# Routed LoRA and expert kernel on Trainium2: the last slot's code in a branch of its own with f32 mixing, W's tile first, and the slots' low parts on VectorE

## The chip, the cores and the metric

The kernel runs on one core of one Trainium2 chip. The metric is the time of one execution on the device in microseconds (us), the median of several runs. Five engines work side by side, each with an instruction queue of its own, and meet by semaphores only: TensorE (PE; PEld is its weight load), VectorE (DVE), ScalarE (ACT), GpSimd (POOL) and the sync engine (SP), which issues most transfers. PEq, DVEq, ACTq, POOLq and SPq stand for the queues themselves, where registers are computed, semaphores waited for and branches taken.

## The reference

The input x holds 32 batches of 64 tokens of 1024 features, f32. Four layers add to it in turn:

```python
x = x + einsum('bct,bcd->bdt', x, W0[cond])           # 16 tables of 64x64, over the 64 tokens
x = x + einsum('bct,bcd->bdt', x, W1[cond])           # the same kind of table
x = x + x @ W.T + (x @ A[labeler]) @ Bw.T * 0.5       # a 1024x1024 base and a low-rank part
x = x + einsum('bsi,boi->bso', x, weight[adapter])    # one of 8 matrices of 1024x1024 for each batch
```

The tables mix tokens and the matrices mix features, so both mixings commute with the feature layers: the kernel computes layers 3 and 4 on the raw x and mixes the 64 tokens of each batch last, with one 64x64 table per condition, (I+W0)(I+W1). Every f32 operand is cut in a high and a low part of reduced precision (`F32R`, fast on TensorE), and a product is three matmuls: high by high, high by low, low by high.

## The kernel before

**Start and base layer.** Transfers bring x and W in tiles of 128 rows. ScalarE writes the high part of each (`x_hi`, `w_hi`), VectorE the low part (`x_lo`, `w_lo`: tile minus high part, L831 and L838). For the first block this goes tile by tile: in the SP block the tile of x is issued before that of W (L281, L282), ScalarE makes `x_hi` then `w_hi` (L595, L597), VectorE adds the unit matrix to a block of W (L1086), then `x_lo`, then `w_lo`. TensorE warms up with `WARM` = 20 matmuls (L1257), computes the table of mixings from f32 operands of 64 rows (L1265), then layer 3 (`main`, L1286 to L1288, one line for each of the three products).

**A plan made on the chip.** VectorE sorts the batches by adapter and packs two batches of the same adapter in a slot. A word per slot in `plan` holds its batches, whether it has a single one (`SINGLE`), whether adapter tiles are to be loaded in it and where. There are between `SURE` = 16 and `SLOTS` = 20 slots; the number is read at run time as `n_slots`. For these inputs it is 17, and slots 4 and 16 hold a single batch.

**Slots.** For slot i the engines do, in `step(i)`:
- ScalarE: `rows_hi(i-1)` (high part of the last slot's result, L694), `slot_hi(i+1)` (high part of the next slot's x, L685), `adapter_part` (high parts of up to 8 adapter tiles, L671), `mixed_cols(i-1)` (L706).
- VectorE: `rows_lo(i-1)` (L1166), `adapter_part` (low parts, L1149), `mixed_sum(i-1)` (L1177).
- GpSimd: `slot_lo(i+1)`, the low part of the next slot's x (L429, two of 128x512), then `mixers(i)` (L443, L445), then the unit matrix on adapter tiles that have landed (L421).
- TensorE: eight tiles of 128 rows, each three products (two for a single slot) for each of two halves of 512 columns (L1400). Between the halves of the tiles comes `mix(i-1)` (L1427), the token mixing of the slot before: four matmuls, for two tables and two halves. Each part stands in `pe.If(single < 1)` / `pe.Else()` (L1411, L1431), so the code of both kinds of slot lies in the queue, one behind the other.
- SP: the transfers of adapter tiles (L332), then `store(i-1)` (L351).

**Slots from `ENDS` = 15 on** can be the last one. TensorE then goes half by half of the columns: all tiles of the first half, `mix(i-1)`, seven tiles of the second (`MIX_AT`), `mix_last(i, 0)` if this is the last slot, the eighth tile, and after the last slot `mix_last(i, 1)` (L1446). `mix_last` needs high and low parts of the slot's result: `last_hi` (L769) on ScalarE and `last_lo` (L1214) on VectorE, two each for a half. Its products are gathered by `last_cols` (L798) and `last_sum` (L1236), and stored in halves of columns and of rows from SP (L368) and ScalarE (L785). Work for slots that may not exist stands in nested branches:

```python
for i in range(SURE, SLOTS):
    with pe.If(n_slots == i):
        mix_last(i - 1, earlier[2], 1)
    nested.enter_context(pe.If(n_slots > i))     # L1489; DVE L1245, ACT L808, SP L394, POOL L496
    earlier, mine = slot(i, earlier, mine)
```

With 17 slots the first of these conditions holds and the second does not: the queue jumps over the code of slots 17, 18 and 19 to the end. Behind its own jump SP waits for every store, L401 and L403. What lies at L248 is the end of a queue's program, with a drain.

## Time and profile before

| | |
|---|---|
| time, median of 3 runs | 394.82 us (394.56 to 395.0) |
| profiled execution | 394.66 us, span of its instructions 392.9 us |
| TensorE, VectorE, ScalarE, GpSimd busy | 380.2, 268.3, 231.2, 123.3 us |
| start to first product; slots; after the last slot's products | 0 to 9.5; 186.9 to 382.5; 382.5 to 392.9 us |
| granted TensorE clock, mean | 0.992 |

The span runs from the first to the last instruction of the traced program. All times of rows are in us from its start, durations marked as such in ns. In a timeline or chain row the first number is the start, the second the time until the last instruction of the group ends; `x4` is the number of instructions. Matmuls overlap each other in such rows: a row's length is more than their number times the step from one to the next. `[3.30 <-DVE aT L1214]` says that the engine was idle for 3.30 us before the row and which instruction ended that. A row of a source line lists durations as min/median/max in ns.

### The profile page before, as it was taken

To read this page: it belongs to the slowest core of one execution; us is meant where nothing else is said; L and a number is where in the kernel's file an instruction comes from. 1 tells how busy PE (TensorE), PEld (TensorE's weight loads), DVE (VectorE), ACT (ScalarE), POOL (GpSimd) and SP (SyncE) were. 2 spreads that over 40 slices of the span, in tenths; PEclk is the share of its full clock that TensorE was granted. 3 is DMA by queue.
4 is the path that set the end of the run, shared out by engine and by line. 5 is a ranking of instruction groups with operands and counts; after the bars stand their busy time and mean duration, and the time that the engine had idled before them with its cause. 6 is when DMAs were issued, how large, how long until landed. Compare 5 with 4: busy or idle time off the path is not lost.

```text
span 392.9 us, 7604 instructions
## 1 busy us (share of the span) xinstructions
PE 380.2 (97%) x1736; PEld 316.4 (81%) x1736; DVE 268.3 (68%) x285; ACT 231.2 (59%) x307; POOL 123.3 (31%) x163
## 2 busy tenths in 40 slices
PE   8999999999999999999999999899999999999990
PEld 8888888888888888888888887688888888888860
DVE  4746967865855958547967439953699546899563
ACT  3798859387232775244483549554677357777361
POOL 0000340100003000024865427763258434576400
PEclk9999999999999999999999999999999999999996
DMA  7984902740348475406526224742276322762223
GB/s 225 396 313 158 375 3 79 261 180 19 107 173 288 182 277 166 180 21 214 175 93 221 58 55 123 260 133 55 56 235 211 97 57 56 270 219 54 56 58 88
DMA packets 24219, 61.37 MB, mean 156 GB/s; under 512 B 1938, under 2 KB 2066, under 8 KB 24146
## 3 DMA queue, kind: packets, MB, share of 16 engines
q1 hardware_dynamic: 23808, 60.30, 46.1%
q8 instruction: 28, 0.46, 0.5%
q14 instruction: 45, 0.37, 0.3%
q10 hardware_dynamic: 338, 0.24, 0.2%
HBM read 52.15 MB, written 8.39 MB: 154 GB/s over the span
## 4 chain that ended last, share of the span: by engine, by line
PE 96%; issue 1%; DVE 1%; ACT 0%; POOL 0%; ACTq 0%; DVEq 0%; POOLq 0%
PE ps L1400 44%; PE ps L1286 13%; PE ps L1287 13%; PE ps L1288 13%; PE ps L1427 4%; PE ps L1313 4%; PE ps L1325 2%; PE ps L1257 1%; PE ps L1265 1%; DVE stage L1236 0%; DVE stage L1177 0%; ACT stage L706 0%; DVE aT L1214 0%; PE ps L1446 0%; ACT stage L798 0%
## 5 line engine op out<-in xcount | busy, mean ns | idle before, releaser
L1400 PE MATMUL ps<-ring,aT 128*128 x784 | 180.8, 389 | 0.0
L1400 PEld LDWEIGHTS ps<-ring,aT 128*128 128x128 f32 x784 | 147.1, 188 | 30.8 <-issue 0.4
L1286 PE MATMUL ps<-ring 128*128 128x512 f32 x224 | 88.3, 394 | 0.0
L1287 PE MATMUL ps<-ring 128*128 128x512 f32 x224 | 88.0, 393 | 0.0
L1288 PE MATMUL ps<-ring 128*128 128x512 f32 x224 | 87.9, 392 | 0.0
L429 POOL TENSOR_TENSOR aT<-xT,aT 128x512 fp32r<-128x512 f32 (+1 forms) x36 | 56.3, 1585 | 51.3 <-ACT aT L685 45.2
L1149 DVE TENSOR_TENSOR ring<-raw,ring 128x1024 f32 (+1 forms) x40 | 63.8, 1655 | 5.1 <-ACT ring L671 5.0
L694 ACT ACTIVATE aT<-ps 64x1024 fp32r<-64x1024 f32 x32 | 32.7, 1021 | 48.1 <-PE ps L1400 47.6
L1177 DVE TENSOR_TENSOR stage<-ps,stage 64x1024 f32<-64x1024 f32 x30 | 36.7, 1222 | 26.3 <-ACT stage L706 25.7
L1166 DVE TENSOR_TENSOR aT<-ps,aT 64x1024 fp32r<-64x1024 f32 x32 | 39.1, 1222 | 22.6 <-ACT aT L694 21.9
L1288 PEld LDWEIGHTS ps<-ring 128*128 128x128 f32 x224 | 42.6, 190 | 9.0
L1286 PEld LDWEIGHTS ps<-ring 128*128 128x128 f32 x224 | 42.6, 190 | 8.9
L1287 PEld LDWEIGHTS ps<-ring 128*128 128x128 f32 x224 | 42.6, 190 | 8.7
L706 ACT ACTIVATE stage<-ps 64x1024 f32<-64x1024 f32 x30 | 30.5, 1017 | 23.7 <-PE ps L1427 23.3
L671 ACT ACTIVATE ring<-raw 128x1024 f32 (+1 forms) x40 | 39.4, 1046 | 8.3 <-POOL raw L421 6.0
L562 ACT ACTIVATE xT<-ps 128x512 f32<-128x512 f32 x40 | 22.6, 592 | 23.0 <-PE ps L1288 22.0
L421 POOL TENSOR_TENSOR raw<-raw,eye 128x128 f32<-128x128 f32 x40 | 19.5, 497 | 24.9 <-DMA raw<-w3t 20.1
L451 POOL TENSOR_TENSOR ring_f<-ring_f,eye 128x128 f32<-128x128 f32 x8 | 5.5, 724 | 66.7 <-DVE ring_f L900 49.6
L838 DVE TENSOR_TENSOR ring<-ring_f,ring 128x1024 fp32r<-128x1024 f32 (+1 forms) x20 | 21.9, 1127 | 5.2 <-ACT ring L513 5.1
L513 ACT ACTIVATE ring<-ring_f 128x1024 fp32r<-128x1024 f32 (+1 forms) x20 | 18.5, 965 | 6.8 <-DMA ring_f<-xt 5.1
L451 POOL TENSOR_TENSOR xT<-xT,eye 128x128 f32<-128x128 f32 x4 | 7.6, 1932 | 44.6 <-DVE xT L894 44.6
L685 ACT ACTIVATE aT<-xT 128x512 fp32r (+1 forms) x36 | 19.9, 599 | 2.4 <-DVE xT L911 2.1
(82 smaller groups left out, 314.5 us busy)
## 6 DMA issues: line engine op xcount, KB each, us to landing
raw<-w3t SPq DMA_DIRECT2D x40, 512.0 KB, 4.4
ring_f<-xt SPq DMA_DIRECT2D x8, 1024.0 KB, 7.7
raw<-xt SPq DMA_DIRECT2D x8, 1024.0 KB, 5.1
out<-stage SPq DMA_DIRECT2D x30, 256.0 KB, 3.0
ring_f<-wt SPq DMA_DIRECT2D x4, 1024.0 KB, 7.4
xT<-xt SPq DMA_DIRECT2D x3, 1024.0 KB, 9.5
xT<-wt SPq DMA_DIRECT2D x2, 1024.0 KB, 15.2
ring_f<-xt SPq DMA_DIRECT2D x4, 256.0 KB, 6.4
```

Source lines behind the costliest of these rows:

```text
L429: pool.tensor_tensor(x3_split(i, ks, P + h * T, T), xT[:, ks, bass.ds(which[h] * T, T)], as_f32(x3_split(i, ks, h * T, T)), ALU.subtract). ...
L562: act.activation(dst[:, o, :], ps_l2(phase, j, o), ACT.Copy).then_inc(s(name), 1)
L671: act.activation(dst, adapter_raw(t), ACT.Copy).then_inc(s("w_hi"), 1)
L694: act.activation(r_tile(h)[own, :], acc(i)[own, :, :].rearrange("p a n -> p (a n)"), ACT.Copy)\
L706: act.activation(stage[own, i % 2, :], mixed_ps[h][other, :, :].rearrange("p a n -> p (a n)"), ACT.Copy)\
L1149: dve.tensor_tensor(in_two(unit_of(t, 1)), adapter_raw(t), as_f32(in_two(unit_of(t, 0))), ALU.subtract)\
L1166: dve.tensor_tensor(r_tile(h)[other, :], acc(i)[own, :, :].rearrange("p a n -> p (a n)"), as_f32(r_tile(h)[own, :]), ALU.subtract).then_in ...
L1177: dve.tensor_tensor(dst, mixed_ps[h][own, :, :].rearrange("p a n -> p (a n)"), dst, ALU.add)\
L1286: pe.matmul(dst, hi_of(qw)[:, k, cs], hi_of(qx)[:, k, :], start=start and k == 0, stop=False, skip_group_check=True)
L1287: pe.matmul(dst, hi_of(qw)[:, k, cs], lo_of(qx)[:, k, :], start=False, stop=False, skip_group_check=True)
L1288: last = pe.matmul(dst, lo_of(qw)[:, k, cs], hi_of(qx)[:, k, :], start=False, stop=stop and k == HALF - 1, skip_group_check=True)
L1400: last = pe.matmul(acc(i)[:, n, :], x3_split(i, k, start, P), ring[:, bass.ds(off + (part * D + n * 512), 512)], start=(k == 0 and j == 0) ...
```

## The change

1. **W's tile first.** SP issues the tile of W before that of x, ScalarE makes `w_hi` before `x_hi`, and VectorE `w_lo` before `x_lo`, for the four tiles of the first block.
2. **Low parts of x on VectorE.** `slot_lo` leaves GpSimd. VectorE makes slot 0's in two parts around `c12(1)`, slot 1's behind the first adapter's tiles, and slot i+1's in `step(i)` directly behind `rows_lo(i-1)`.
3. **The last slot in a branch of its own.** On each engine a recursive `rest` replaces the nested branches: `If(n_slots > i+1)` holds the step and all that is deeper, its `Else` the last slot's code. Slot 15 is an ordinary slot when it isn't the last. In the last slot TensorE goes by three parts of the columns (512, 256, 256), once for pairs (`columns(PAIR)`) and once for single slots (`columns(ALONE)`).
4. **f32 mixing of the last slot.** GpSimd puts the tables together in one f32 matrix, ScalarE copies the result in f32 (`last_row`), and one f32 matmul for each part mixes it, with no low parts, column copies or sums behind it. `last_row` lies where the rows of slot i-1 are, so the first copy waits for their mixing. Six matmuls (`BRIDGE`) stand before the last one.
5. **Stores and waits.** In a single last slot there are three stores, of one part each and all rows, the last one from ScalarE. Each `store(i)` waits for `store(i-2)`, and the row of waits at the end goes.

The core of the diff (the same pattern of `rest` on ScalarE and VectorE is left out, and what is only taken away):

```diff
             for k in range(HALF):
                 one = slice(k, k + 1)
+                sp.dma_start(raw_of(w_slot(0))[:, one, :], w_block(1, 1)[:, one, :]).then_inc(s(f"w_in0_{k}"), 16)
                 sp.dma_start(raw_of(x_slot(0))[:, one, :], x_block(1, 0)[:, one, :]).then_inc(s(f"x_in0_{k}"), 16)
-                sp.dma_start(raw_of(w_slot(0))[:, one, :], w_block(1, 1)[:, one, :]).then_inc(s(f"w_in0_{k}"), 16)
...
+    END_COLS = (slice(0, 512), slice(512, 768), slice(768, D))
...
             def store(i, word):
                 rows, single = batches(word), get(word, SINGLE)
+                if i >= 2:
+                    sp.wait_ge(s(f"stored{i - 2}"), 32)
                 sp.wait_ge(s("staged"), 2 * (i + 1))
...
+                sp.wait_ge(s(f"stored{i - 2}"), 32)
                 with sp.If(single < 1):
...
                 with sp.Else():
-                    first = slice(0, T // 2)
-                    for n in range(2):
-                        sp.wait_ge(s("end_staged"), n + 1)
-                        sp.dma_start(out_half(rows[0], n, first), stage[first, i % 2, 512 * n:512 * (n + 1)]).then_inc(s("end"), 16)
+                    for part in range(2):
+                        sp.wait_ge(s("end_out"), part + 1)
+                        store_part(0, part, "end")
+                sp.wait_ge(s(f"stored{i - 1}"), 32)
...
-            for i in range(SLOTS - 1):
-                if i < SURE - 1:
-                    sp.wait_ge(s(f"stored{i}"), 32)
-                else:
-                    with sp.If(n_slots > i + 1):
-                        sp.wait_ge(s(f"stored{i}"), 32)
-            sp.wait_ge(s("end"), 64)
+            def rest(i, word):
+                if i == SLOTS:
+                    store_last(i - 1, word)
+                    return
+                with sp.If(n_slots > i):
+                    rest(i + 1, step(i, word))
+                with sp.Else():
+                    store_last(i - 1, word)
+            rest(SURE, word)
+            sp.wait_ge(s("end"), 48)
...
         def _(pool):
+            def mixers_last(word):
...
+                with pool.Else():
+                    whole(slice(0, P), cs[0], slice(0, T)).then_inc(s("end_st"), 3)
...
         def _(act):
+            def last_rows(i, part):
+                act.wait_ge(s("end_left"), part + 1)
+                act.activation(last_row[:, END_COLS[part]], end_acc(i, part), ACT.Copy).then_inc(s("end_rows"), 1)
+            def last(i, earlier, word):
+                rows_hi(i - 1)
+                act.wait_ge(s("mixed"), i)
+                last_rows(i, 0)
+                mixed_cols(i - 1, earlier)
+                last_rows(i, 1)
+                last_rows(i, 2)
+                act.wait_ge(s(f"stored{i - 2}"), 32)
+                act.wait_ge(s("end_mixed"), 3)
+                act.activation(stage[:, i % 2, END_COLS[2]], end_ps(i, 2), ACT.Copy).then_inc(s("end_out2"), 1)
+                act.wait_ge(s("end_out2"), 1)
+                act.dma_start(out_part(batches(word)[0], 2), stage[0:T, i % 2, END_COLS[2]]).then_inc(s("end"), 16)
...
         def _(dve):
             adapter_lo((0, HALF), 0, lambda t, part: unit(KT + t, part))
-
+            word = slot_word(dve, 0)
+            slot_lo(0, word, (0, HALF))
             c12(1)
+            slot_lo(0, word, (HALF, KT))
             adapter_lo((HALF, KT), 0, lambda t, part: unit(t - HALF, part))
+            slot_lo(1, slot_word(dve, 1))
...
             def step(i, earlier, word):
-                following = slot_word(dve, i + 1) if i + 1 < SLOTS else None
+                following = slot_word(dve, i + 1)
                 if i:
                     rows_lo(i - 1)
+                    slot_lo(i + 1, following)
...
+            def last(i, earlier):
+                rows_lo(i - 1)
+                mixed_sum(i - 1, earlier)
+                dve.wait_ge(s(f"stored{i - 2}"), 32)
+                for part in range(2):
+                    dve.wait_ge(s("end_mixed"), part + 1)
+                    dve.tensor_copy(stage[:, i % 2, END_COLS[part]], end_ps(i, part)).then_inc(s("end_out"), 1)
...
         def _(pe):
+            def mix_last(i, part):
+                pe.wait_ge(s("end_st"), 3)
+                pe.wait_ge(s("end_rows"), part + 1)
+                pe.matmul(end_ps(i, part), last_mix[:, :], last_row[:, END_COLS[part]], start=True, stop=True)\
+                  .then_inc(s("end_mixed"), 1)
...
+                def columns(passes):
+                    end_products(i, mine, passes, 0)
+                    mix(i - 1, earlier[2])
+                    end_products(i, mine, passes, 1)
+                    mix_last(i, 0)
+                    end_products(i, mine, passes, 2, (0, END_AT))
+                    mix_last(i, 1)
+                    end_products(i, mine, passes, 2, (END_AT, KT))
+                slot_ready(i)
+                with pe.If(mine[2] < 1):
+                    columns(PAIR)
+                with pe.Else():
+                    columns(ALONE)
+                warm(BRIDGE, acc(i - 1)[:, 1, 256:512])
+                mix_last(i, 2)
+            def rest(i, earlier, mine):
+                if i == SLOTS - 1:
+                    last_slot(i, earlier, mine)
+                    return
+                with pe.If(n_slots > i + 1):
+                    rest(i + 1, *slot(i, earlier, mine))
+                with pe.Else():
+                    last_slot(i, earlier, mine)
...
-            for i in range(SURE):
+            for i in range(ENDS):
                 earlier, mine = slot(i, earlier, mine)
...
+            rest(ENDS, earlier, mine)
```

`PAIR` is ((0, 0), (0, 1), (P, 0)), `ALONE` ((T, 0), (T, 1)), `END_AT` 6.

## Rows read from the trace of the kernel before

**Rows 1.** The page, part 1: busy time, share of span and number of instructions.

```profile
PE 380.2 (97%) x1736; PEld 316.4 (81%) x1736; DVE 268.3 (68%) x285; ACT 231.2 (59%) x307; POOL 123.3 (31%) x163
```

**Rows 2.** Waits of PE: in total, times, longest, us.

```profile
PE ps L1427 <- issue: 1.8, 3, 1.5
```

**Rows 3.** Timeline of PE from 370 us on: start, length, instructions, idle time before.

```profile
377.24 1.18 PE L1427 MATMUL ps<-aT,st 128*128 128x512 f32 x4 [0.17 <-issue]
378.26 3.35 PE L1400 MATMUL ps<-ring,aT 128*128 x14
...
385.81 0.85 PE L1446 MATMUL ps<-aT,st 128*128 128x512 f32 x2 [3.30 <-DVE aT L1214]
```

**Rows 4.** The same view for all engines, 364 to 393 us: ScalarE and VectorE.

```profile
378.51 1.21 ACT L769 ACTIVATE aT<-ps 64x512 fp32r<-64x512 f32 x2 [2.97 <-PE ps L1427]
...
379.75 2.07 ACT L706 ACTIVATE stage<-ps 64x1024 f32<-64x1024 f32 x2
380.81 2.48 DVE L1177 TENSOR_TENSOR stage<-ps,stage 64x1024 f32<-64x1024 f32 x2 [0.26 <-ACT stage L706]
```

**Rows 5.** SP's last stores by source line: durations, first and last start; time to landing.

```profile
L368 SPq DMA_DIRECT2D out<-stage x2: 342/362/381, 385.9 to 388.4; - x2
...
DMA to landing us min/median/max: 2.5/2.7/2.8
```

**Rows 6.** Branches, SP's waits and its drain, by source line.

```profile
L1489 PEldq COMPARE_BRANCH  x2: 68/2034/3999, 370.3 to 385.8; - x2
...
L394 SPq COMPARE_BRANCH  x2: 40/45/50, 374.3 to 388.8; - x2
...
L401 SPq EVENT_SEMAPHORE  x7: 28/28/28, 391.3 to 391.7; - x7
...
L248 SPq DRAIN  x1: 13/13/13, 392.7 to 392.7; - x1
```

**Rows 7.** Timeline of the start, VectorE and PE.

```profile
5.92 3.68 PE L1265 MATMUL ps<-stage 64*128 64x64 f32 x32
...
8.37 0.69 DVE L831 TENSOR_TENSOR ring<-ring_f,ring 128x512 fp32r<-128x512 f32 x1
...
9.53 0.79 PE L1286 MATMUL ps<-ring 128*128 128x512 f32 x1
```

**Rows 8.** Timeline of VectorE, low parts of adapter tiles in slots 4 and 14.

```profile
237.67 5.75 DVE L1149 TENSOR_TENSOR ring<-raw,ring 128x1024 f32 x4 [0.83 <-ACT ring L671]
...
354.41 6.88 DVE L1149 TENSOR_TENSOR ring<-raw,ring 128x1024 f32 x4
```

**Rows 9.** Timeline of PE: matmuls of 256 columns at the full clock.

```profile
137.45 4.00 PE L1313 MATMUL ps<-ring,a_sel 128*128 128x256 f32 x32
```

**Rows 10.** The tensor queue in 366 to 371, 354.9 to 357.9, 371 to 374 us.

```profile
L1411 PEldq COMPARE_BRANCH  x5: 65/179/292, 366.8 to 370.7; - x5
...
L1400 PEldq FUSED_REGOPS  x16: 46/46/51, 355.3 to 357.5; - x16
...
L1400 PEldq FUSED_REGOPS  x16: 42/46/51, 371.3 to 373.9; - x16
```

**Rows 11.** The chain that ended last: start and length of slot 14's and 15's products.

```profile
356.22 10.88 PE ps L1400 x48
```

**Rows 12.** Transfers of PE's instructions (q8), 255 to 360, 387 to 388, 390 to 391 us.

```profile
q8 instruction: 10, 0.16, 0.6%
...
q8 instruction: 1, 0.02, 5.8%
...
q8 instruction: 1, 0.02, 7.5%
```

**Rows 13.** Timeline of VectorE before slot 15's rows.

```profile
374.53 2.48 DVE L1166 TENSOR_TENSOR aT<-ps,aT 64x1024 fp32r<-64x1024 f32 x2 [2.74 <-ACT aT L694]
```

**Rows 14.** PE at 14.3 us; one microsecond by engine, clock after POOL, DMA share, GB/s.

```profile
14.32 0.40 PE L1288 MATMUL ps<-ring 128*128 128x512 f32 x1
...
386.00:387.00 1.00, 0.66 (x2) 0.10 (x1) 0.00 (x0) 0.13 (x1) 0.00 (x0) 0.64 0.89 275
```

More of the change, by code:

```diff
@@ L242, in build, with out_part @@
     BEFORE3, WBASE = HALF, HALF * OPERANDS
-    def out_half(row, n, rows=slice(0, T)):
-        return out[bass.ds(row, 1), rows, 512 * n:512 * (n + 1)].rearrange("a t d -> (a t) d")
+    def out_part(row, part, rows=slice(0, T)):
+        return out[bass.ds(row, 1), rows, END_COLS[part]].rearrange("a t d -> (a t) d")
     with nc.Block() as block:
@@ L489, in step, with rest @@
                 return word, following
+            def rest(i, earlier, word):
+                if i == SLOTS - 1:
+                    mixers_last(word)
+                    return
+                with pool.If(n_slots > i + 1):
+                    rest(i + 1, *step(i, earlier, word))
+                with pool.Else():
+                    mixers_last(word)
             earlier = None
-            for i in range(SURE):
+            for i in range(ENDS):
                 earlier, word = step(i, earlier, word)
-            with contextlib.ExitStack() as nested:
-                for i in range(SURE, SLOTS):
-                    nested.enter_context(pool.If(n_slots > i))
-                    earlier, word = step(i, earlier, word)
+            rest(ENDS, earlier, word)
         @block.scalar
@@ L771, in last @@
-            def last(i, word):
-                rows, single = batches(word), get(word, SINGLE)
-                last_cols(i, single, 0)
-                last_hi(i, 1)
-                last_cols(i, single, 1)
-                with act.If(single < 1):
-                    for n in range(2):
-                        act.wait_ge(s("end_staged"), 2 * n + 2)
-                        act.dma_start(out_half(rows[1], n), stage[T:P, i % 2, 512 * n:512 * (n + 1)]).then_inc(s("end"), 16)
-                with act.Else():
-                    second = slice(T // 2, T)
-                    for n in range(2):
-                        act.wait_ge(s("end_staged"), n + 1)
-                        act.dma_start(out_half(rows[0], n, second), stage[second, i % 2, 512 * n:512 * (n + 1)]).then_inc(s("end"), 16)
@@ L1250, in _, with rest @@
+            def rest(i, earlier, word):
+                if i == SLOTS - 1:
+                    last(i, earlier)
+                    return
+                with dve.If(n_slots > i + 1):
+                    rest(i + 1, *step(i, earlier, word))
+                with dve.Else():
+                    last(i, earlier)
+            earlier = None
+            for i in range(ENDS):
+                earlier, word = step(i, earlier, word)
+            rest(ENDS, earlier, word)
         @block.tensor
@@ L1387, in slot_record, with products @@
                         get(word, SINGLE))
-            def products(i, mine, passes, tiles, ns, first):
+            def products(i, mine, passes, tiles):
                 count8, offs, _ = mine
@@ L1473, in slot, with end_products @@
                     mix(i - 1, earlier[2])
-                    slot_part(i, mine, (0, MIX_AT), (1,), False)
-                    with pe.If(n_slots == i + 1):
-                        mix_last(i, mine[2], 0)
-                    slot_part(i, mine, (MIX_AT, KT), (1,), False)
+                slot_part(i, mine, (HALF, KT))
                 return mine, following
+            def end_products(i, mine, passes, part, tiles=(0, KT)):
+                count8, offs, _ = mine
+                cols = END_COLS[part]
+                for k in range(*tiles):
+                    if part == 0:
+                        pe.wait_ge(s("w_lo"), count8 + (k + 1 + WBASE - KT))
+                    off = offs[k // HALF] + (k % HALF) * UNIT
+                    for j, (start, split) in enumerate(passes):
+                        last = pe.matmul(end_acc(i, part), x3_split(i, k, start, P),
+                                         ring[:, bass.ds(off + (split * D + cols.start), cols.stop - cols.start)],
+                                         start=(k == 0 and j == 0), stop=(k == KT - 1 and j == len(passes) - 1))
+                if tiles[1] == KT:
+                    last.then_inc(s("end_left"), 1)
```

223 lines of the change are left out of this document (72 added, 151 removed).

## The prediction

> **What bounds the kernel now.** I read the page first: the matmul engine is busy for 380.2 of 392.9 us [rows 1], so only its idle stretches and what lies after its last instruction can be won. The waits name 1.8 us ahead of the slots' mixing, 1.5 of them in one piece [rows 2]. The timeline of the end has the rest: products and mixing run nearly without a gap up to 382.5 (after the row at 378.26 come two mixing matmuls and the last two products), then TensorE idles 3.3 us until two matmuls at 385.81 [rows 3]. In that pause ScalarE and VectorE make high and low parts of the last 512 columns, in turns, as the pair at 378.51 shows for the first 512 [rows 4]. Last, the sync queue: its last store is issued at 388.4 and lands some 2.7 us later, at about 391.1 [rows 5]. The span goes on to 392.9, and the branch records tell why: after the branch over the unused slots (L394, 388.8) the next instruction starts at 391.3. This 2.5 us is no wait for data; the seven waits there take 28 ns each. The tensor queue has such a branch too, L1489: 68 ns when it falls through, 3999 ns when it jumps over the three unused slots [rows 6]. A far jump costs 2.5 us on SP and 4.0 us on PE. Today all of them are taken after the last work.
>
> The profiled execution took 394.66 us, span 392.9 and 1.8 around it, 0.16 under the median of 394.82. I sum changes of the span and add them to the median.
>
> **The start.** W's tile first swaps two pairs of equal steps: the second low part still ends at about 9.06 (8.37 and 0.69). The first product starts at 9.53, when the mixing table's f32 matmuls are through (5.92 and 3.68), and not for it [rows 7]: cover 0.5 us, cost 0.0.
>
> **The slots.** A low part of 128x512 costs VectorE 0.69 us [rows 7], so a slot adds 1.38 us there, behind `rows_lo`, ahead of adapter tiles and of `mixed_sum`. Most slots have that room. The tight ones are those with four adapter tiles. In slot 4 these ran from 237.67 for 5.75 us (1.24 each where nothing disturbs, as the sums of [rows 4], 5.0 in all), and the chain behind them gave the 1.5 us stall. There VectorE had idled 0.83 us, so the cost is 0.55 us less contention that leaves with GpSimd's work, at most 0.8. In slot 14 no idle time precedes the group and it takes 6.88 us [rows 8]; 1.38 come in, up to 1.9 go out, but GpSimd's casts move forward into it. I take 0 for both; ends -0.3 and +1.3.
>
> **The tail, code at hand.** The last slot is a single one: 16 products of one half (14 and 2 around the mixing in [rows 3]). Part 0 and the mixing of slot 15 stay as they are, ending at 378.26. Part 1 is 16 matmuls of 256 columns, 0.125 each (4.00/32) [rows 9]: 380.3. The f32 mixing matmul is not in the trace at this size. Nearest is L1265: 32 of 64 rows and 64 columns in 3.68 us at the half clock [rows 7]. If two half-height ones run side by side, 512 columns of full height cost 0.92 us at the full clock; the other end is 0.23, as the reduced-precision ones. I take 0.92, and 0.46 for 256: 381.2. Twelve products, the second mixing and four products: 383.6. ScalarE copies 256 columns in 0.38 (0.60 for 512, 1.03 for 1024, [rows 4]): 384.2 with 0.2 to start. Last mixing with 0.35 ahead: 385.0; copy 385.6; issued 385.8, landed 388.5, end 388.9. This replaces 385.81 to 388.2 and removes two low parts, two sums and 1.2 us of waits on SP. The six bridging matmuls (0.75) lie in ScalarE's copy.
>
> SP has a longer chain. Slot 15's sums ended at 383.29; ScalarE now has one copy of 0.59 ahead of them, not 1.21: 382.67. From there to SP's first last store were 2.6 us (two stores of slot 15) [rows 4, 5]. **But the branch over unused slots now stands before `store_last`, since that is in its `Else`, behind all deeper slots' code.** With 2.55 us for it the first store goes at 387.8, the second at 388.3, lands at 391.0, end 391.4: 1.5 us better than 392.9.
>
> **The same branch on PE.** In slot 15, after the mixing, the tensor queue begins the second half at 366.8 [rows 10]. A half of 24 products passes the queue in 3.1 us (355.3 to 357.5 for its address steps, and the branches around them), so it reaches the branch at 370.0, 3.4 us ahead of the engine: 24 x 0.227 (10.88/48, [rows 11]), from 368.0 behind the four mixing matmuls at 367.1, ends at 373.4. The branch takes 4.0 us [rows 6]: 374.0. From a branch to the first product's address step were 1.0 us (370.3 to 371.3) [rows 6, 10], and 0.2 to the matmul: 375.2, 1.8 us late.
>
> Then, 0.4 us behind, comes a second jump: over `columns(PAIR)` to `columns(ALONE)`. In the slots blocks of 16 KB of instructions came once in 10.5 us (10 in 105 us) [rows 12], and a slot of 11.8 us (10.88 and the mixing's 0.91) holds both branches, 80 products and 8 mixing matmuls. `PAIR` has 72 products and 6 others: some nine tenths of a block. So the target lies nearly always in the next block. After the jump at 385.8 the next block began to come only between 390 and 391 [rows 12], 4.8 us after the branch, 0.8 after PE went on. The first block's transfer began between 387 and 388 [rows 12], and PE went on at 389.8, so a block is ready some 2.3 us after its transfer begins. That makes about 7.3 us after the first branch: 377.3; with 0.7 for the address steps and the load, first product 378.0, 4.6 us late. The ends: the block is there (1.8 late), or a full load of 4.0 from 374.4 (5.7 late). I take 4.6, which follows the only far jump in the trace.
>
> On this the Trainium skill speaks against the change: "Runtime: NRT & Kernel Launch", section "Instruction fetch mechanics", says that a taken branch to outside the two loaded pages stalls until its page has come. By that both of PE's jumps are charged. The trace agrees for the first, with 3999 ns. The same section gives PE 128 KiB; if that much were kept ahead, the second would be free, which is the first rival.
>
> The other engines take the jump in idle time: VectorE idles 2.74 us before slot 15's rows at 374.53 [rows 13], ScalarE waits for the same products before them, and what GpSimd has to make is due at 380.
>
> **The clock.** TensorE stood 3.3 us before 385.81, and within the next microsecond the granted clock fell from 2.4 GHz to 1.2 GHz, 0.64 on the mean [rows 14]. A pause of 4.6 us is longer. At the start the first product took 0.79 at 9.53 and one took 0.40 at 14.3 [rows 7, 14]: half rate for 4.8 us, 2.4 us lost. So the last slot loses between 0 and 2.4 us; I take 1.0, as it may not fall, and what it costs behind slot 15's mixing is hidden by SP's chain, 2.5 us longer than PE's.
>
> **The sum.** Mixing of slot 15 starts at 381.6 (378.0 + 16 x 0.227), not 377.24: 4.4 late. SP's chain 391.4 + 4.4 + 1.0 = 396.8, against 392.9: +3.9, **398.7 us**.
>
> **The rivals.** (a) One load: PE's second jump finds its block. 1.8 late at the first product, 1.6 at the mixing: 391.4 + 1.6 = 393.0, time 394.9. For it: jumps over half a slot cost 0.07 to 0.3 us throughout. Against: these blocks had long been loaded.
> (b) The other side: no load delays PE, because the queue runs far enough ahead. SP's alone remains: 391.4, time 393.3. It decides at 2.2 us: a branch that costs less than that leaves the engine fed. Against it: 4.0 in the only row; for it: at 370 no transfers stand before the block, at 386 stores did.
> (c) The change does as it says, no load in any path: 388.9, time 390.8. It needs SP's 2.5 us gone too.
> (d) Two full loads and a clock that falls: +1.1 and +1.4 on the forecast, 401.2. For it: the jump may start its own load.
> (e) VectorE as the bound in slots: +1.3 at most, on top of any.
> The point between slower and faster is a mixing of slot 15 that starts 1.5 us late (392.9 - 391.4).
>
> **How the numbers follow.** Two loads 0.60 (with (d)), one load 0.14, (b) 0.17, (c) 0.06, the rest something else. A measurement tells 0.2%, 0.8 us, from no change. (a) lies within it with its spread of 0.8 to each side: half of its chance same, the rest to both sides. Faster 0.27, same 0.10, slower 0.63. The range leaves out (c) and the top of (d): 392.8 to 400.6. The likeliest case alone: 396.8 to 401.2.
>
> **What would show it.** Right: a branch in the tensor queue of some 4 us at about 370, the matmul engine idle from 373.4, a second long one at the branch between `PAIR` and `ALONE`; SP's 2.5 us now between slot 15's stores and the last ones; the granted clock below 1 in the last slot. The 1.5 us stall in slot 5 about as long as now. Wrong: no idle time at 373, both branches below 0.4 us; then (b) or (c). Wrong in size: f32 mixing matmuls of 0.25 us, or a stall ahead of the mixing of slots 4, 9 or 14 that grew.

## The result and the profile after

The changed kernel takes 399.96 us, median of four runs (399.79 to 400.22), against 394.69 us before (393.79 to 395.0): the ratio is 1.0144, its 95% interval 1.0128 to 1.0161. It is slower, by 5.3 us. The profiled execution took 400.01 us, its span is 398.2 us. Nearly all of the loss lies behind the last products of slot 15: from the mixing of slot 13 to the end of the span it is 37.75 us before (355.15 to 392.9) and 42.92 after (355.28 to 398.2).

The page, part 1, columns as in [rows 1]:

```profile
PE 380.3 (96%) x1760; PEld 316.7 (80%) x1760; DVE 269.9 (68%) x317; ACT 229.6 (58%) x305; POOL 64.1 (16%) x125
```

GpSimd has lost half its work and VectorE has gained only 1.6 us. The waits of PE, where [rows 2] had 1.5 us in one piece:

```profile
PE ps L1462 <- issue: 4.8, 1, 4.8
PE ps L1319 <- DVE low_split L926: 1.7, 1, 1.7
...
PE ps L1419 <- issue: 1.1, 2, 0.9
PE ps L1280 <- DVE ring L840: 1.0, 1, 1.0
PE ps L1419 <- POOL st L456: 0.9, 1, 0.9
```

The first is new: 4.8 us in which the matmul engine waits "for issue", that is for its own queue. The waits at L1319, L1280 and for GpSimd (L456) are new too; they lie at the start and in slot 0, and the points on the start and the slots below come back to them. The timeline of the end shows the place, to be held against [rows 3] and [rows 4]:

```profile
378.38 5.49 PE L1462 MATMUL ps<-ring,aT 128*128 x16 [4.81 <-issue]
...
383.71 1.07 PE L1419 MATMUL ps<-aT,st 128*128 128x512 f32 x4
...
386.49 2.48 DVE L1191 TENSOR_TENSOR stage<-ps,stage 64x1024 f32<-64x1024 f32 x2 [9.36 <-ACT stage L734]
386.53 1.02 PE L1434 MATMUL ps<-last_row,last_mix 128*128 128x512 f32 x2
...
388.82 0.59 PE L1434 MATMUL ps<-last_row,last_mix 128*128 128x256 f32 x2
389.00 1.02 DVE L1227 COPY stage<-ps 128x512 f32<-128x512 f32 x2
...
390.45 0.67 PE L1434 MATMUL ps<-last_row,last_mix 128*128 128x256 f32 x2
391.22 0.38 ACT L796 ACTIVATE stage<-ps 128x256 f32<-128x256 f32 x1 [0.91 <-PE ps L1434]
391.78 0.58 ACTq L798 DMA_DIRECT2D out<-stage  x1
394.98 1.33 SPq L376 DMA_DIRECT2D out<-stage  x2
```

The mixing of slot 15 starts at 383.71 instead of 377.24. What TensorE and the copies do behind it is short: the last copy is done at 391.6. But the last two stores leave SP only at 394.98. The branches say why (durations min/median/max in ns, first and last start), the counterpart of [rows 6]:

```profile
L1492 PEldq COMPARE_BRANCH  x2: 76/2450/4823, 358.0 to 369.6; - x2
...
L1481 PEldq COMPARE_BRANCH  x1: 3158/3158/3158, 374.8 to 374.8; - x1
...
L1494 PEldq COMPARE_BRANCH  x1: 3939/3939/3939, 390.5 to 390.5; - x1
...
L418 SPq COMPARE_BRANCH  x2: 40/42/45, 373.9 to 391.0; - x2
...
L379 SPq ALU_OP  x2: 37/37/37, 394.4 to 394.5; - x2
```

L1492 is `If(n_slots > i + 1)`: 76 ns where it falls through, 4823 ns where it jumps to the last slot's code. L1481 is the jump over `columns(PAIR)`: 3158 ns. L418 is the same on SP: its record is short, but the next instruction of SP starts at 394.4, so the jump took 3.4 us, while the data of both stores lay ready (VectorE's copies end at 390.0). Last, PE in stretches (busy and instructions, granted clock, DMA share, GB/s):

```profile
374.00:378.00 4.00, 0.00 (x0) 1.00 0.39 109
378.00:380.00 2.00, 1.62 (x4) 0.67 0.03 8
380.00:382.00 2.00, 2.00 (x6) 0.50 0.00 0
382.00:384.00 2.00, 2.00 (x10) 0.98 0.00 0
```

After the pause TensorE runs at 1.2 GHz (0.50) and comes back to 2.4 GHz around 382: 6 matmuls in the two microseconds from 380, 10 in the next two.

### The profile page after: what moved, and what is told of

Its sections match the earlier page's. It is cut to its first block, busy times and chain, and to the rows that moved or that the text cites. A ratio compares the mean times of both kernels' runs of the same rounds, so it can differ in the third digit from the quotient of the medians.

```text
span 398.2 us, 7647 instructions
## 1 busy us (share of the span) xinstructions
PE 380.3 (96%) x1760; PEld 316.7 (80%) x1760; DVE 269.9 (68%) x317; ACT 229.6 (58%) x305; POOL 64.1 (16%) x125
## 4 chain that ended last, share of the span: by engine, by line
PE 83%; ACT 4%; DVE 4%; DMA 3%; issue 2%; POOL 1%; ACTq 1%; SPq 0%; POOLq 0%; DVEq 0%
PE ps L1393 39%; PE ps L1280 11%; PE ps L1281 11%; PE ps L1282 11%; PE ps L1419 4%; PE ps L1307 3%; PE ps L1462 2%; PE ps L1319 2%; DMA ring_f<-xt 1%; DMA raw<-w3t 1%; ACT ring L541 1%; ACT ring L538 1%; DVE ring L1151 1%; DVE aT L1180 1%; ACT a_sel L570 1%
## 5 line engine op out<-in xcount | busy, mean ns | idle before, releaser
L1393 PE MATMUL ps<-ring,aT 128*128 x752 | 173.1, 389 | 0.0
L1393 PEld LDWEIGHTS ps<-ring,aT 128*128 128x128 f32 x752 | 141.1, 188 | 29.4 <-issue 0.2
L1280 PE MATMUL ps<-ring 128*128 128x512 f32 x224 | 87.4, 390 | 1.0 <-DVE ring L840 1.0
L722 ACT ACTIVATE aT<-ps 64x1024 fp32r<-64x1024 f32 x32 | 32.7, 1022 | 48.0 <-PE ps L1393 47.6
L1280 PEld LDWEIGHTS ps<-ring 128*128 128x128 f32 x224 | 42.1, 188 | 9.7 <-issue 1.1
L1282 PEld LDWEIGHTS ps<-ring 128*128 128x128 f32 x224 | 42.1, 188 | 8.8
L1281 PEld LDWEIGHTS ps<-ring 128*128 128x128 f32 x224 | 42.1, 188 | 8.6
L1151 DVE TENSOR_TENSOR ring<-raw,ring 128x1024 f32 (+1 forms) x40 | 47.2, 1241 | 0.1
L441 POOL TENSOR_TENSOR raw<-raw,eye 128x128 f32<-128x128 f32 x40 | 21.4, 539 | 87.8 <-DMA raw<-w3t 87.3
L1160 DVE TENSOR_TENSOR aT<-xT,aT 128x512 fp32r<-128x512 f32 (+1 forms) x36 | 23.2, 685 | 1.2 <-ACT aT L713 0.7
L454 POOL CAST st<-aT 128x64 fp32r x32 | 12.6, 393 | 48.4 <-issue 20.6
L570 ACT ACTIVATE a_sel<-a_tab 128x512 fp32r x32 | 18.8, 626 | 1.5 <-issue 1.2
```

What stands on the lines that cost most here:

```text
L570: act.activation(a_sel[:, pair % SEL, :, h, :, :].rearrange("p k t r -> p k (t r)"), as_f32(a_tab[:, bass.ds(l, 1), :, :, :].rearrange("p ...
L722: act.activation(r_tile(h)[own, :], acc(i)[own, :, :].rearrange("p a n -> p (a n)"), ACT.Copy)\
L1151: dve.tensor_tensor(in_two(unit_of(t, 1)), adapter_raw(t), as_f32(in_two(unit_of(t, 0))), ALU.subtract)\
L1160: dve.tensor_tensor(x3_split(i, ks, P + h * T, T), xT[:, ks, bass.ds(which[h] * T, T)], as_f32(x3_split(i, ks, h * T, T)), ALU.subtract).t ...
L1280: pe.matmul(dst, hi_of(qw)[:, k, cs], hi_of(qx)[:, k, :], start=start and k == 0, stop=False, skip_group_check=True)
L1281: pe.matmul(dst, hi_of(qw)[:, k, cs], lo_of(qx)[:, k, :], start=False, stop=False, skip_group_check=True)
```

## The experiments

Times are medians; each ratio is against the kernel before. As kernels with the same code up to slot 13 reach it up to 2 us apart, I also give, as **tail**, the time from the mixing of slot 13 to the end of the profiled span, which leaves that out: 37.75 before, 42.92 after. It is good to some 0.5 us: slot_lo and w_first, whose end is that of the kernel before, have 38.25 and 38.2.

**pe_near, all_near.** TensorE alone, then all engines, without code for slots 17 to 19:

```diff
             def rest(i, earlier, mine):
-                if i == SLOTS - 1:
+                if i == 16:
                     last_slot(i, earlier, mine)
                     return
```

> The changed kernel, but on TensorE alone the branches end at slot 16, so the code for more than 17 slots is left out there and no far jump stands in front of the last slot's products (SyncE, ScalarE and VectorE keep theirs). Theory (the far jump on TensorE's queue is paid in front of the last slot, and the jump over the pair's code is then covered by the products of slot 15): first product of the last slot near 373.6 instead of 378.4, the clock stays full, the mixing of slot 15 near 377.2 to 378.9 instead of 383.7; SyncE's own jump of 3.4 us stays between the stores of slot 15 and the last ones, so the time is 393.3 to 394.5. Rival (the second jump waits for its code as long as before, so only one of two waits goes): first product near 375 to 376.7, time 396 to 397.5. Rival (VectorE's low parts of x hold the last slot, not the code): time stays at 399 to 400.

> The changed kernel with the branches ended at slot 16 on all five engines: the code for more than 17 slots is left out, so no engine jumps far in front of its last work; stores, f32 mixing, waits, the loads at the start and the low parts on VectorE stay. Theory (code loads on TensorE and SyncE are all that the change lost): 390.5 to 391.5, that is 3.3 to 4.3 below the kernel before, and 2.5 to 3 below the kernel in which only TensorE's jump is gone. Rival (SyncE's jump lies beside other work once TensorE is early): same as that kernel, 393.3 to 394.5. Rival (f32 mixing and the new order cost as much as the stores save): 394.5 to 395.

Measured: pe_near 393.07 us (ratio 0.9966, 0.9955 to 0.9978), tail 37.16; all_near 390.69 us (0.9896, 0.9878 to 0.9915), tail 34.22. Both theories hold, pe_near's 0.2 us below its range (its profiled execution took 394.07). The timeline of pe_near (PE) and the branch over the pair's code, then PE's timeline and SP's last stores in all_near:

```profile
373.27 3.79 PE L1462 MATMUL ps<-ring,aT 128*128 x16
377.22 1.19 PE L1419 MATMUL ps<-aT,st 128*128 128x512 f32 x4 [0.17 <-issue]
...
L1481 PEldq COMPARE_BRANCH  x1: 2240/2240/2240, 369.8 to 369.8; - x1
```

```profile
373.61 3.79 PE L1462 MATMUL ps<-ring,aT 128*128 x16
377.56 1.18 PE L1419 MATMUL ps<-aT,st 128*128 128x512 f32 x4 [0.16 <-issue]
...
L376 SPq DMA_DIRECT2D out<-stage x2: 474/667/860, 385.6 to 386.6; - x2
```

With the far jump gone, products run on without a pause, though L1481 still takes 2.24 us: the queue was that far ahead of the engine, so this jump was free. The first 16 products take 3.79 us instead of 5.49: the half-rate stretch cost 1.70 us. Pause and clock, 5.0 and 1.7, are what TensorE lost. The tail shows 5.76 of these 6.7: in the changed kernel the last stores landed 2.1 to 2.3 us after issue, here after 2.7 to 2.8. Without SP's jump the tail is 2.94 shorter again, and the first of the last stores leaves at 385.6, 1.6 us behind VectorE's copies instead of 5.0. all_near is 4.0 us faster than the kernel before, but not all of this is the change's: it also lacks the far exit jump of SP, which the kernel before has. Little code is left behind the last slot here, that of slot 15's own last-slot version, and the jump over it at TensorE's end still took 4.0 us:

```profile
L1492 PEldq COMPARE_BRANCH  x2: 68/2038/4007, 358.2 to 384.4; - x2
```

That is as long as the exit jump over three slots in the kernel before (3999 ns), so the length of a jump alone doesn't set its price.

**pe_one_jump.** The far jump kept, the one over the pair's code gone:

```diff
                 slot_ready(i)
-                with pe.If(mine[2] < 1):
-                    columns(PAIR)
-                with pe.Else():
+                if i == 16:
                     columns(ALONE)
+                else:
+                    with pe.If(mine[2] < 1):
...
```

> The changed kernel, in which TensorE's last slot at slot 16 has the code for a single batch only, so the jump over the pair's code is gone and the far jump to the last slot is kept (the kernel then serves 17 slots with a single batch last). Theory (two loads one behind the other, 4.8 and 3.2 us, of which 4.8 is idle time in front of the products): first product near 374.9 instead of 378.4, no or little half-rate clock, time 394.8 to 396.5. Rival (the second jump is short once the first block has come, and the 3.2 us is something else, such as the wait for slot 16's inputs): no change, 399.5 to 400.

Measured: 393.47 us (0.9977, 0.9963 to 0.9991), 1.3 below the theory's range; tail 38.22, 4.70 shorter. PE's branch and timeline:

```profile
L1495 PEldq COMPARE_BRANCH  x2: 68/2394/4719, 356.0 to 367.6; - x2
...
372.87 3.92 PE L1462 MATMUL ps<-ring,aT 128*128 x16 [1.29 <-issue]
```

One far jump leaves 1.29 us of pause, not 4.81, and the 16 products take 3.92, with a granted clock of 1.00 from 373 to 377. So the second jump cost 3.5 us of pause, and the half rate came with the longer pause only: 5.1 us, of which SP's chain shows 4.7. The median lies 6.5 us below the changed kernel, because this kernel was also 2.0 us earlier at slot 13 (353.28, not 355.28). That part isn't the jump's, and the theory's range had left it out: 1.9 of it are there at the mixing of slot 0, at 203.89 in the changed kernel behind the wait of 0.9 us for GpSimd, and here, without that wait, at

```profile
201.99 1.10 PE L1419 MATMUL ps<-aT,st 128*128 128x512 f32 x4
```

**swapped.** All code kept, the two sides of each branch exchanged on every engine (TensorE's shown):

```diff
-                with pe.If(n_slots > i + 1):
-                    rest(i + 1, *slot(i, earlier, mine))
-                with pe.Else():
+                with pe.If(n_slots < i + 2):
                     last_slot(i, earlier, mine)
+                with pe.Else():
+                    rest(i + 1, *slot(i, earlier, mine))
```

> The changed kernel with the two sides of each branch exchanged on every engine, so that the code of the last slot stands first: with 17 slots each engine jumps over the last slot's code of a 16-slot plan when slot 15 begins, and falls into the last slot without a jump. Theory (a far jump costs the same wherever it stands on TensorE, which is busy throughout; on SyncE, ScalarE and VectorE it is covered in slot 15): TensorE loses 4 to 5 us near 356 and the jump over the pair's code is then covered by slot 15's products; SyncE's 3.4 us before the last stores is gone; time 394 to 396.5. Rival (the jump in slot 15 is covered by TensorE's queue of issued work, since the queue runs some us ahead there): 391 to 392. Rival (a jump at each of the two places, as now): 399 to 400.

Measured: 392.87 us (0.9959, 0.9946 to 0.9972), tail 37.09. The time fell into the theory's range, but for another reason. The branch on PE (three of it), PE's timeline, and SP's stores and branches in swapped:

```profile
L1492 PEldq COMPARE_BRANCH  x3: 68/2916/4370, 356.1 to 382.7; - x3
...
371.84 3.79 PE L1462 MATMUL ps<-ring,aT 128*128 x16
...
L376 SPq DMA_DIRECT2D out<-stage x2: 485/850/1214, 384.1 to 384.8; - x2
...
DMA to landing us min/median/max: 3.1/3.1/3.1
...
L418 SPq COMPARE_BRANCH  x3: 38/40/45, 372.4 to 387.1; - x3
...
L260 SPq COMPARE_BRANCH  x1: 43/43/43, 390.1 to 390.1; - x1
```

The jump at the start of slot 15 (356.1, 2.9 us) costs TensorE only 0.3 us: counted from slot 13, the first product of the last slot starts at 18.43 us (371.84 - 353.41), in all_near at 18.13. The rival was right about that, though its time, 391 to 392, was too low. What held the end was SP again: it has issued its last store by 386.0, waits inside the branch for slot 15's stores until 387.1, then jumps out over the code of the deeper slots and goes on at 390.1, when the stores (3.1 us after 384.8) had landed for 2 us. A far jump had only changed places with the stores.

**slot_lo, w_first.** The kernel before with one part of the change each, as in the diff above.

> The kernel before with one part of the change alone: the low parts of x for each slot on VectorE instead of GpSimd. Theory (VectorE has room in every slot, and the mixers on GpSimd only gain): 394.4 to 395.0, within 0.2 percent of before; the stall in front of the mixing of slot 0, 0.9 us in the changed kernel, shows here too if it comes from the order on GpSimd, and the stall in slot 5 shrinks by about as much. Rival (VectorE holds the products of a slot): 395.6 to 396.1. Rival (it gives 1 to 2 us back, since low parts on GpSimd slowed VectorE through memory they share: VectorE's low parts of the adapters fell from 1655 to 1241 ns each in the changed kernel): 392.7 to 394.

> The kernel before with one part of the change alone: W's tile before x's in the loads of the first slot and on ScalarE and VectorE. Theory (the products of the start wait for both tiles of a pair in any case): 394.4 to 395.0, within 0.2 percent of before. Rival (the split of the tile with W's identity comes earlier and the start gets 0.4 to 1.2 us shorter): 393.5 to 394.3.

Measured: slot_lo 394.1 us (0.9982, 0.9963 to 1.0), w_first 394.86 us (1.0004, 0.9994 to 1.0013). W's tile first changes nothing above 0.5 us. The low parts on VectorE gain perhaps 0.7 us, at the edge of what 12 runs can tell; the median is 0.3 below the theory's range. The wait for GpSimd ahead of slot 0's mixing doesn't show here. The trace of slot_lo shows where the gain lies, to be held against [rows 8] and the 1.46 us stall of [rows 2]:

```profile
236.40 1.29 DVE L1142 TENSOR_TENSOR aT<-xT,aT 128x512 fp32r<-128x512 f32 x2
237.71 4.63 DVE L1133 TENSOR_TENSOR ring<-raw,ring 128x1024 f32 x4
...
247.74 1.19 PE L1428 MATMUL ps<-aT,st 128*128 128x512 f32 x4 [0.87 <-issue]
```

1.29 us come in, 0.83 us of idle time and 1.12 us of the adapter's low parts go out (5.75 to 4.63), so the stall shrinks by 0.6. All 40 of these low parts together took 63.8 us in the kernel before, 47.6 here:

```profile
L1133 DVE TENSOR_TENSOR ring<-raw,ring 128x1024 f32 (+1 forms) x40 | 47.6, 1248 | 0.1
```

That is 16 us of VectorE given back for 22.5 us of new work: VectorE was slower on such tiles while GpSimd made x's low parts beside it.

**in_place, in_place_all.** The rest of the change put into the old, nested branches, where the queue falls into its last slot, in two halves of the columns; then with both small parts added:

```diff
             def mix_last(i, single, n):
-                pe.wait_ge(s("st"), 4 * (i + 1))
-                pe.wait_ge(s("end_lo"), 2 * n + 2)
...
+                pe.wait_ge(s("end_st"), 3)
+                pe.wait_ge(s("end_rows"), n + 1)
+                pe.matmul(end_ps(i, n), last_mix[:, :], last_row[:, 512 * n:512 * (n + 1)], start=True, stop=True)\
+                  .then_inc(s("end_mixed"), 1)
...
             def store_last(i, word):
...
+                sp.wait_ge(s(f"stored{i - 1}"), 32)
```

> The kernel before with the nested branches kept as they are, so every engine falls into its last slot without a far jump, but with the change's single-pass f32 mixing of the last slot in two halves, its copies instead of copies and additions, and SyncE's waits for old stores taken before new ones. The low parts stay on GpSimd. It serves all numbers of slots. Theory (the arrangement of the branches is what lost the time, the rest of the change gains): 390.5 to 391.5. Rival (the gain of the kernel without far code came from its three unequal parts and the bridging products, not from f32 mixing): 392.5 to 394. Rival (nothing gained, SyncE's exit jump of 2.5 us sets the end): 394 to 395.

> The previous kernel (nested branches kept, f32 mixing in halves) with the other two parts of the change added: low parts of x on VectorE and W's tile first. Theory (both are worth nothing): the same as the previous one within 0.5 us, 390.5 to 391.5. Rival (they gain or lose where the single kernels say so): the previous kernel's time plus the two differences measured alone.

Measured: in_place 393.63 us (0.9974, 0.996 to 0.9989), tail 36.43; in_place_all 392.14 us (0.9944, 0.9922 to 0.9965), tail 36.23. I expected 390.5 to 391.5 for both and missed it by over 2 us and by 0.6. In in_place TensorE did its part; SP's records show something I had overlooked:

```profile
L399 SPq COMPARE_BRANCH  x2: 38/39/40, 384.2 to 387.9; - x2
...
L251 SPq COMPARE_BRANCH  x1: 43/43/43, 390.8 to 390.8; - x1
```

The change's last wait, for slot 15's stores, stands inside the branch. It holds SP until 387.9, and only then comes the exit jump, until 390.8. In the kernel before no wait for these stores stood ahead of that jump. The small parts gained 1.5 us more, with 0.2 of it in the tail; their sum measured alone would be 0.3 (medians of 394.61 before, 394.1 for slot_lo, 394.86 for w_first). The two profiled executions are only 0.7 us apart (392.99 and 392.33), so the rest of the 1.5 isn't explained.

**swapped_ends, in_place_ends.** That wait taken out of the branch, in both arrangements. The stores of the last slot but one count on the semaphore that SP waits for after its jump (swapped_ends shown; in in_place_ends, which is in_place_all with this edit, the count is 96):

```diff
-                sp.wait_ge(s(f"stored{i - 1}"), 32)
...
-                if i:
+                if i >= ENDS:
+                    with sp.If(n_slots == i + 1):
+                        store(i - 1, earlier, "end")
+                    with sp.Else():
+                        store(i - 1, earlier)
+                elif i:
                     store(i - 1, earlier)
...
-            sp.wait_ge(s("end"), 48)
+            sp.wait_ge(s("end"), 80)
```

> The kernel with exchanged branch sides (last slot's code first, all numbers of slots served), in which SyncE no longer waits for slot 15's stores inside the branch: these stores count on the semaphore that is waited on after SyncE's exit jump, so that this jump of 2.9 us runs while the last stores land. Theory (in the kernel with exchanged sides the exit jump after a wait satisfied at 387.1 set the end at 390.1, while PE's last mixing was done at 383.3): end 1.0 to 1.5 us earlier, time 391.2 to 391.9. Rival (the last stores themselves land only at 390, held up by the code that all engines load for their exit): no change, 392.6 to 393.1.

> The kernel with nested branches kept, f32 mixing in halves, low parts on VectorE and W first, with the same edit on SyncE: slot 15's stores are waited for after the exit jump. Theory: SyncE's exit jump starts at 386.3 instead of 387.6 and ends at 389.0; end 0.9 to 1.2 us earlier, time 390.9 to 391.4. Rival (the last stores land at 390 anyway): no change, 392.0 to 392.4.

Measured: swapped_ends 390.87 us (0.9905, 0.9886 to 0.9924), tail 35.85; in_place_ends 391.41 us (0.9924, 0.9909 to 0.994), tail 35.92. SP's branches in swapped_ends:

```profile
L388 SPq COMPARE_BRANCH  x1: 38/38/38, 386.0 to 386.0; - x1
...
L260 SPq COMPARE_BRANCH  x1: 43/43/43, 388.7 to 388.7; - x1
```

In swapped_ends the jump and the landing of the last stores now lie side by side, 2.7 us for the jump, and the tail is 1.2 us shorter (37.09 to 35.85); the median is 0.3 us below the theory's range. In in_place_ends the median comes out at the range's upper edge, but the tail is only 0.3 us shorter (36.23 to 35.92):

```profile
L375 SPq DMA_DIRECT2D out<-stage x2: 336/484/632, 384.3 to 385.1; - x2
...
DMA to landing us min/median/max: 2.3/3.1/3.9
```

Its second store, issued at 385.1, landed up to 3.9 us later, at 389.0, and SP goes on at 389.1: there the landing took the place of the jump, as the rival had it. So the wait inside the branch explains 1.2 us in one arrangement and 0.3 in the other, and the 2 us that in_place missed stay in part open. The rival for in_place, that all_near's gain came from the three unequal parts and the bridging products, isn't borne out: two halves and three parts end with the same tail (35.92 and 35.85). TensorE's jump at the start of slot 15 cost 0.6 us in swapped_ends (first product of the last slot at 18.70 from slot 13). swapped_ends serves every number of slots and beats both kernels, the kernel before by 3.7 us and the changed one by 9.1; in_place_ends, 0.5 us slower with overlapping intervals, can't be told from it. Only inputs with 17 slots were timed: with more slots swapped_ends takes one such jump in every further slot.

**no_bridge, swapped_best.** all_near with `BRIDGE` = 0; and swapped_ends with `BRIDGE` = 0 and with slot 0's mixing matrices made ahead of the second adapter's identities:

```diff
+                mixers(i, word)
                 if i == 0:
                     with pool.If(n_active > 1):
                         adapter_eyes(0, 1)
-                mixers(i, word)
```

> The kernel without far code on any engine (no code for more than 17 slots), with the six bridging products of the last slot left out, against 390.69 with them. Theory (they only fill TensorE's wait for ScalarE's last copy and the clock holds over 0.9 us without them): 390.4 to 390.9, the same. Rival (TensorE falls to half rate without them and the last f32 mixing of 0.67 us doubles, or they are long enough to delay it): 391.2 to 391.5, or 390.0 to 390.2.

> The kernel with exchanged branch sides and SyncE's late waits, with two more edits: on GpSimd slot 0's mixing matrices are made before the identities are added to the second adapter's tiles (in the changed kernel they come behind four transfers of that adapter, and the mixing of slot 0 waited 0.9 us for them in some profiles and not in others), and the six bridging products are left out. Theory (the wait before the mixing of slot 0 is GpSimd's order, and it is what spreads runs of one kernel by 1 us): no wait there in the profile, time 390.0 to 390.7, against 390.87, with a narrower spread. Rival (the adapter's tiles come later and stall slot 5 by as much more): 390.7 to 391.2.

Measured: no_bridge 389.94 us (0.9879, 0.9862 to 0.9896), tail 34.56 against all_near's 34.22; swapped_best 391.01 us (0.9909, 0.9885 to 0.9934), tail 35.70. TensorE without the bridging products, in no_bridge:

```profile
381.47 0.82 PE L1462 MATMUL ps<-ring,aT 128*128 x4
382.86 0.67 PE L1434 MATMUL ps<-last_row,last_mix 128*128 128x256 f32 x2 [0.56 <-ACT last_row L783]
```

From the last products to the last mixing are 1.39 us (382.86 - 381.47), and it takes 0.67 us, both as with the bridge (390.45 - 389.06 and 0.67 in the changed kernel). The six matmuls do nothing. The median lies 0.5 us below the theory's range and below all_near's, but that isn't from the tail: slot 13 came 1.5 us earlier (353.94, not 355.48). swapped_best lies in its rival's range, with the stall in slot 5 as before (0.85 us). The wait in front of slot 0's mixing is not there in it, but swapped_ends had none in its profile either, and the time is the same; the spread (390.8 to 392.18) is no narrower. The theory that this wait makes the spread isn't borne out.

## Why the prediction was right, point by point

The forecast was 398.7 us and slower, by two loads of code in front of TensorE's last slot and one in front of SP's last stores. The mechanism is as forecast: taking out one jump after the other gives back its part. The point between slower and faster, slot 15's mixing 1.5 us late, was passed by far: it is 6.5 us late.

- **First branch on TensorE.** Forecast at 370.0 for 4.0 us; it came at 369.6 and took 4.8. The row it was priced from, 3999 ns, was a branch over three slots; the exit jump of this kernel passes only slot 15's last-slot code and took 3939 ns. TensorE's exit jumps in the kernels of this text take 3.7 (in_place_ends) to 4.5 us (in_place_all), all less than the jump in front of the last slot.
- **Second branch.** Forecast: waits for its block until 377.3, first product 378.0. It took 3.16 us until 377.9, first product 378.38. The size is right, the reason only half: I had the second block come by itself behind the first, some 7.3 us after the first branch. Two blocks came around the first branch and one only behind the second, between 375 and 376 us. The two rows that follow are the transfers of PE's instructions in 370 to 371 and in 375 to 376:

```profile
q8 instruction: 1, 0.02, 14.9%
...
q8 instruction: 1, 0.02, 6.2%
```

  The branch began at 374.8, so the second jump waited for a load that began after it. This was the mechanism of rival (d), and that the size came out right is partly luck (the working also rounds up: 4.8 and 2.3 us are 7.1, not 7.3). By the Trainium skill, "Runtime: NRT & Kernel Launch", section "Instruction fetch mechanics", a taken branch out of the two pages held stalls for a fetch. The trace agrees, at 4.8 and 3.2 us; the 128 KiB that the section gives PE did not spare the second.
- **The clock.** I took 1.0 out of 0 to 2.4. It was 1.70 (5.49 against 3.79), and nothing behind the 1.29 us pause of pe_one_jump, where the granted clock stayed at 1.00. This is the largest miss on TensorE, 0.7 us.
- **SP's jump.** Forecast 2.55, from the exit jump before; it was 3.4. The stores landed 2.1 to 2.3 us after issue, not 2.7, which gives 0.4 to 0.6 back. The clock's 0.7, the first product's 0.4 and this jump's 0.85, less that 0.5, are the 1.4 us by which the span's end, 398.2, lies behind the forecast 396.8; that the first three were all taken a little low is what puts the time at the upper end of the range.
- **f32 mixing.** Forecast 0.92 for 512 columns and 0.46 for 256. The chain that ended last in no_bridge has

```profile
379.10 0.86 PE ps L1434 x2
379.96 1.43 PE ps L1462 x12
381.39 0.43 PE ps L1434 x2
```

  which is 0.86 and 0.43. The estimate was close; whether two half-height matmuls run side by side, as it assumed, no run shows.
- **The tail with code at hand.** Forecast 388.9 for the span (rival (c), 390.8); all_near measured 389.7 and 390.69. Rival (b), SP's jump alone, 393.3; pe_near measured 393.07. As tails these forecasts are 33.75 and 36.25 and the profiles show 34.22 and 37.16, so the second agreement, within 0.3 us in time, is partly luck.
- **The start.** 0.0 forecast, 1.0004 measured for w_first. The cover I named was thinner than it looked: it was the mixing table's matmuls at half rate. The clock came up earlier in the profile after, they took 2.32 us instead of 3.68, and the first product then waited 1.0 us for VectorE's low part. At its first low-rank products (L1307, 25.72, against L1313, 28.18) the changed kernel was 2.5 us ahead; then came the 1.7 us wait for VectorE at L1319, and at the second ones, 48.90 against 49.27, 0.4 were left.
- **The slots.** I took 0, ends -0.3 and +1.3. slot_lo shows a gain of 0.6 in slot 5, where the stall shrank from 1.46 to 0.87 (0.9 in the changed kernel too) and I had it about as long as before: past my lower end. In the changed kernel a wait of 0.9 us for GpSimd ahead of slot 0's mixing took more than that back. I had not seen this one: `mixers(0)` stands behind transfers of adapter tiles. It shows in the profiles of pe_near and all_near too and is missing in those of slot_lo, pe_one_jump and swapped, so the code alone doesn't decide it; that it goes with when these land is a guess. That start and slots together put slot 13 at 355.28, against 355.15, is several such terms cancelling: luck, not the forecast zero.

Slot 13 is reached up to 2.3 us apart in kernels with much the same code up to there, and the profiles divide this. From the second low-rank products to the mixing of slot 13 are 305.9 us with the low parts on GpSimd (before, w_first, in_place), 305.2 to 305.3 with them on VectorE, and 306.3 to 306.4 in the three profiles with the wait for GpSimd (the changed kernel, pe_near, all_near). The rest, up to 1.4 us, comes before those products. The changed kernel and pe_one_jump:

```profile
48.90 4.00 PE L1307 MATMUL ps<-ring,a_sel 128*128 128x256 f32 x32
```

```profile
48.06 4.00 PE L1307 MATMUL ps<-ring,a_sel 128*128 128x256 f32 x32
```

So of the 2.0 us between these two, 0.8 are the start's and 1.2 come with the wait. Each is one profiled execution. What makes the start's length, and with it some of the differences between medians that the tails don't show, stays open.

## What to carry to other kernels

A branch costs by whether its target's code is there, and on SP its own record doesn't show it: with `If(more): ... Else: last`, the last work stands behind all the code that is not run, and here TensorE paid 4.8 and 3.2 us and SP 3.4 us in front of it. Let the queue fall into its last work, or take the jump a slot earlier, while the engine still has issued work (0.3 to 0.6 us lost here); and after the last store, jump first and wait then. If a kernel has an exit jump at the end of a queue, it gives a first price for such an edit, here 0.8 to 0.9 us too low.

## What I had not expected of the hardware

- A taken branch of `rest` cost 4.7 to 4.8 us on TensorE in front of the last slot, over three slots, and 2.9 to 3.2 us at the start of slot 15 in the swapped kernels, over one last slot's code. As an exit jump that same short distance took 3.9 to 4.3 us (the changed kernel, pe_near, all_near, no_bridge). SP's far jumps took between 2.5 and 3.4 us.
- The branch over the pair's code took 2.24 and 2.60 us in kernels without any far jump ahead of it (pe_near, all_near), but 0.33 in swapped: a jump over 72 products, fewer than a slot's code has, may wait for code or not, and no run shows what decides it. It didn't show in the time, because TensorE had work for longer.
- With the low parts of x on GpSimd, VectorE's of the adapter took a third longer: 1655 ns on the mean before, 1248 in slot_lo.
- The last mixing after a pause of 0.56 us takes no longer than after bridging products, and a pause of 1.29 us leaves the clock at 2.4 GHz, while one of 4.81 us didn't.
